# The order of weighing, projections and scores in a layer's attention

## The reference, cut to what matters

```
qkv = shift_tokens(x) @ Wqkv                 # 128 -> 3 * 1024: 16 heads of 64
q, k = l2norm(q) * qs, l2norm(k) * ksc       # then a rotation (rotary tables)
sim = einsum(q, k of this and the previous window of 32) * 8
attn = softmax(masked sim)
x = (attn @ v) @ Wo + x
x = ffn_layer(shift_tokens(x)) + x           # not touched
```

## Time and profile before

| what | us |
|---|---|
| median of 3 timed runs | 5682.57 |
| lowest, highest | 5681.54, 5702.88 |
| the profiled execution's own time | 5641.73 |
| its span, first to last instruction | 5639.9 |

### The profile page before, as it was taken

The page is one execution under the profiler, slowest core; times in us unless marked ns, Lnnn a source line. Parts: engine busy times, 40 slices in busy tenths (PEclk is TensorE's granted clock), DMA queues, the critical chain, the costliest instruction groups (busy, mean ns, idle before and its releaser), DMA issues. The chain is left out here.

```text
span 5639.9 us, 183409 instructions
## 1 busy us (share of the span) xinstructions
PE 4558.5 (81%) x70227; PEld 3064.2 (54%) x70227; DVE 3371.8 (60%) x7024; ACT 2396.0 (42%) x5161; POOL 2573.2 (46%) x4541
## 2 busy tenths in 40 slices
PE   8999838668888878888888888877788887888885
PEld 6777616544555545555555555555555555555553
DVE  3555441666666666665666666666566665666665
ACT  4555443124444344443444444444434444344441
POOL 0000000107666366663566645656546665366661
PEclk9999869879999999999999999989999999999998
DMA  1000003011111010101110111110101011011100
GB/s 34 4 4 3 1 0 98 6 37 28 26 25 29 24 33 22 29 22 30 26 29 22 28 30 26 24 27 22 37 19 29 22 28 37 19 24 27 28 22 31
DMA packets 76047, 143.02 MB, mean 25 GB/s; under 512 B 19655, under 2 KB 57749, under 8 KB 68117
## 3 DMA queue, kind: packets, MB, share of 16 engines
q1 hardware_dynamic: 75284, 131.92, 9.5%
HBM read 35.40 MB, written 4.19 MB: 7 GB/s over the span
## 5 line engine op out<-in xcount | busy, mean ns | idle before, releaser
L2439 DVE TENSOR_TENSOR n_tt<-n_pp,n_rot 128x1024 f32<-128x1024 f32 x768 | 923.4, 1222 | 693.4 <-ACT n_sq L2307 690.5
L1941 POOL TENSOR_TENSOR n_pre<-n_tt 128x512 f32<-128x512 f32 x768 | 969.9, 1274 | 802.8 <-DVE n_tt L2439 802.6
L2057 PE MATMUL n_pp<-n_wqkv,n_xT 128*128 128x512 f32 x1536 | 811.8, 631 | 6.3 <-ACT n_xT L2302 5.6
L2312 ACT COPY n_V<-n_pp 128x512 f32<-128x512 f32 x384 | 224.7, 585 | 1391.1 <-PE n_pp L2065 1391.1
L1976 POOL TENSOR_TENSOR n_pre<-n_pre,n_rn 128x512 f32<-128x512 f32 x768 | 776.6, 1042 | 36.8 <-POOL n_rn L1964 36.8
L2108 PE MATMUL n_pS<-n_qkT 64*32 64x64 f32 (+1 forms) x24576 | 359.4, 233 | 362.9 <-issue 362.9
L2307 ACT ACTIVATE n_sq<-n_pp 128x512 f32<-128x512 f32 x768 | 457.0, 595 | 158.5 <-PE n_pp L2057 152.8
L2108 PEld LDWEIGHTS n_pS<-n_qkT 64*32 64x32 f32 x24576 | 294.5, 110 | 396.2 <-issue 396.2
L2446 DVE TENSOR_REDUCE n_ss<-n_sq 128x8 f32<-128x512 f32 x768 | 504.2, 676 | 0.0
L2065 PE MATMUL n_pp<-n_wqkv,n_xT 128*64 128x512 f32 x1536 | 484.4, 760 | 0.0
L2074 PE MATMUL n_pp<-ident,n_pre 128*128 128x128 f32 x3072 | 420.7, 280 | 72.2 <-POOL n_pre L1976 70.2
(11 more groups left out here) (263 smaller groups left out, 7918.6 us busy)
## 6 DMA issues: line engine op xcount, KB each, us to landing
n_Vx<-n_V SPq DMA_DIRECT2D x192, 256.0 KB, 3.9
n_Vx<-n_V SPq DMA_DIRECT2D x192, 192.0 KB, 3.2
n_wqkv<-in_L_ffn_Wqkv SPq DMA_DIRECT2D x6, 1536.0 KB, 7.4
e_w<-in_L_ffn_w SPq DMA_DIRECT2D x32, 256.0 KB, 3.0
m_Y<-e_ye SPq DMA_DIRECT2D x64, 64.0 KB, 2.0
n_wo<-in_L_ffn_Wo SPq DMA_DIRECT2D x6, 512.0 KB, 7.2
a_xs<-in_L_attn_x SPq DMA_DIRECT2D x16, 128.0 KB, 2.1
x_kept<-X SPq DMA_DIRECT2D x1, 2048.0 KB, 8.6
```

The lines of the kernel that those rows point to most:

```text
L1941: nc.gpsimd.tensor_tensor(d, s[0], s[1][:, :, ::-1, :], ALU.add).then_inc(s_add, 1)
L2057: nc.tensor.matmul(pp[:, c % 2, :], xT[:, j * P:(j + 1) * P], wqkv[:, t * I + 512 * half:t * I + 512 * half + 512], start=True, stop=True) ...
L2439: nc.vector.tensor_tensor(tt[:, c % 4, :, :].rearrange("p s (h d) -> p s h d", d=D), bcast(pp[:, c % 2, :].rearrange("p (h d) -> p h d", d ...
```

## The change

In a half visit where the next visit exists (`nxt`), TensorE does weighing, two q/k projections, the wait for the turned q and k, two V projections and then the scores. The wait for `s_qkT` moves behind masks, weighing and the q/k projections there. ScalarE does both squares first, then the two V copies and the two exponentials. VectorE does the two rotations and one sum of squares ahead of the maxima, the second sum of squares behind them, and adds y to X after that. The number of instructions that compute is the same, GpSimd's and SyncE's lists are as before, and so are the banks.

```diff
--- before.py
+++ after.py
@@ -2173,18 +2173,20 @@
                         weights_ready(pairs[0], N, u, 0)
                     elif prev:
                         weights_ready(pairs[0], N - 1, 1 - u, 1)
-                    after(pe, s_qkT, 8 * N + 4 * j + 4)
+                    if not nxt:
+                        after(pe, s_qkT, 8 * N + 4 * j + 4)
                     masks(N, j)
                     if j == 1:
                         weigh(u, 0)
                     elif prev:
                         weigh(1 - u, 1)
-                    scores(j)
                     if nxt:
+                        project_qk(N + 1, 4 * j)
+                        project_qk(N + 1, 4 * j + 1)
+                        after(pe, s_qkT, 8 * N + 4 * j + 4)
                         project_v(N + 1, 2 * j, bank("v", 2 * j, 1))
                         project_v(N + 1, 2 * j + 1, bank("v", 2 * j + 1, 1))
-                        project_qk(N + 1, 4 * j)
-                        project_qk(N + 1, 4 * j + 1)
+                    scores(j)
                     if prev:
                         output(N - 1, j, bank("y", j, -1))
                     if j == 1:
@@ -2353,14 +2355,12 @@
 
                 for j in range(2):
                     if nxt:
+                        square(N + 1, 4 * j)
+                        square(N + 1, 4 * j + 1)
                         copy_v(N + 1, 1 - u, 2 * j, bank("v", 2 * j, 1))
                         copy_v(N + 1, 1 - u, 2 * j + 1, bank("v", 2 * j + 1, 1))
                     exps(N, j, 0)
-                    if nxt:
-                        square(N + 1, 4 * j)
                     exps(N, j, 1)
-                    if nxt:
-                        square(N + 1, 4 * j + 1)
                     if j == 1:
                         copy_output(N, 0, bank("o", 0, 0))
                         copy_output(N, 1, bank("o", 1, 0))
@@ -2494,15 +2494,15 @@
                         norm_output(N, 0)
                     elif prev:
                         norm_output(N - 1, 1)
-                    maxima(N, j)
                     if nxt:
                         rotate(N + 1, 4 * j)
                         rotate(N + 1, 4 * j + 1)
+                        sum_squares(N + 1, 4 * j)
+                    maxima(N, j)
+                    if nxt:
+                        sum_squares(N + 1, 4 * j + 1)
                     if prev:
                         add_attention(N - 1, b - 1, j, at["y", j, -1][0])
-                    if nxt:
-                        sum_squares(N + 1, 4 * j)
-                        sum_squares(N + 1, 4 * j + 1)
                     sum_exps(N, j)
                     if nxt:
                         for c in (4 * j + 2, 4 * j + 3):
```

## The result

The changed kernel takes 5330.45 us in the median of 4 runs (5325.95 to 5343.95), beside 5688.01 for the kernel before (5681.54 to 5702.88, 4 runs): a ratio of 0.9372, with a 95% interval of 0.9345 to 0.9398. Later, beside three variants on one chip, it took 5333.63 against 5680.34 (0.9391). The forecast was 5440, with 5300 to 5640; the saving is 357 us where 244 were forecast. Between the two profiled executions it is 316 us (5641.73 to 5325.95).

The account below looks back on a forecast made before the run. The prediction took TensorE's instruction supply, one block of 256 every 3.5 to 4 us, to limit the small matmuls. Terms -359 + 165 - 50 = -244 us gave 5440 us, range for 8 in 10: 5300 to 5640.

Parts of the forecast that it names:

- step (1): TensorE's scores: dense projections between weighing and scores remove the instruction-supply gap in 174 half visits, -359 us.
- C: Third of a loop iteration's four half visits, full clock and no loop end: 16.95 us before, forecast 15.55.
- step (2): TensorE's second turned output: new wait for VectorE's X, about 0.95 us in each half visit, 165 us lost.
- step (3): VectorE: two rotations and a sum of squares fit ahead of the maxima, 0.1 to 0.2 us to spare; cost nothing.
- The rival of the late maxima: VectorE's chain becomes the path: maxima 1 us late add 174 us, 5610; chance 0.13, plus 0.07 for over 1.2 us.
- step (4): ScalarE's squares first, earlier q/k projections, SyncE's copies and POOL (GpSimd): each costs nothing.
- step (5): TensorE's clock: B's low-clock loss of 1.3 us in each of 36 iterations goes, about -50 us; A's stays.
- B: Second of a loop iteration's four half visits, 20.97 us before, clock share 0.92; forecast to reach granted clock 1.00.
- A: First of a loop iteration's four half visits, behind the idle loop end, 20.17 us before; low-clock loss forecast unchanged.
- D: Fourth of a loop iteration's four half visits, 21.13 us before; gap in the scores forecast to go there too.

Follow-up runs that it names:

- run 72: Not a run number: 72 us is what adding y to X ahead of the second sum of squares saved against the changed kernel; 5261.86 us, ratio 0.9261.
- half of this change alone: Only TensorE's order changed against the kernel before, with VectorE and ScalarE keeping theirs: 5957.41 us, ratio 1.0512.
- one overlooked copy: Changed kernel with output y behind the turned outputs, so y waits for a ScalarE copy standing behind both exponentials: 5794.85 us, ratio 1.0198 to the kernel before.

## Why the prediction was right

**The supply gap, step (1).** Right, and shown by taking it away with useless work. I forecast -359 us, from the weight loads' idle time; the matmuls' own fell by 362.9 - 25.0 = 338, and that is what TensorE lost. Of the weight loads' own 396, 173 us are left at no cost to the matmuls. The count of 174 came out by luck: the change is in all but the last two half visits of a layer, and the first had no gap to lose.

The rule that I set against it stands in the Trainium skill, "Runtime: NRT & Kernel Launch", section "Instruction fetch mechanics": crossing a block is mostly hidden. For a run of small matmuls the traces do not agree: there are 2.1 us at C's crossing, and 1.7 us of filler take 363 us of such gaps down to 49. The same section of the Trainium skill says that a taken branch to code outside the two blocks at hand waits for a fetch. The trace agrees: with the loop written out, 90.2 us of idle time in 30 places go, 3.0 us each.

**The wait for X, step (2).** Right in mechanism; the path was not what I said. In C the second turned output was to start at 3.5 us and starts at 3.46; C was to take 15.55 us and takes 15.41. But I had all of the wait on the path, and in C hardly any of it is: with X earlier the wait fell by 0.6 us and C by 0.11. C's length is near the forecast because another chain, GpSimd's among it, ends there almost as late. Over the run 72 of 99 us came through. The waits themselves grew by 129 us (165.2 - 35.8) where I said 165.

**VectorE's cover, step (3).** It holds. From the masks the sum ends at 6.70 us (I said 6.8) and the scores at 7.11 (6.90), so there are 0.4 us to spare where I had 0.1 to 0.2, and VectorE waits 0.54 us where I gave 0 to 0.3. The sum itself took 0.68, not 0.60. The rival of the late maxima did not happen. That the other engines' orders are needed for it, the run of TensorE's order alone shows: 12% between them.

**ScalarE, SyncE, GpSimd, step (4).** Nothing in sum, as forecast, though not in each place: the turned weights in a layer's first visit wait 27 us for exponentials, which I had left out, and the wait of turned q and k for GpSimd fell by as much (70.2 to 41.8). And GpSimd's room in C was smaller than its busy time says: with four of its steps left out C falls, so the chain is on C's path, while its small chained steps idle between each other.

**The clock, step (5), mis-sized.** I gave 50 us for B and left A. The low level lost 948 - 713 = 235 us of time. The weighing's gaps fell by 10 us (91.6 to 81.2). What is left of the 316 us after the waits (316 - 338 + 129 - 10) is 97. TensorE's busy time for the same matmuls fell by about as much, 101.5 us (4558.5 to 4457.0), so most of the 97 is likely the clock; no run measures it apart. In B the granted clock was 0.92 and is 1.00, as I said, and A is still in part at the low level (0.75, now 0.83). I had sized B by one iteration. In the mean of 36, B spent 4.3 us at the low level before and none after, A 6.7 and 5.4, and the half visits at the start of a layer and D gave back some as well.

**A wait moved, not in my sum.** I had the gap in B's weighing stay at 1.44 us. It is 0.32 in the iteration shown, and in the mean 0.62 where it was 1.57; in D, where it was 0.11, it grew to 0.48, so the sum of these gaps hardly changed:

```profile
2251.00 0.30 PE L2133 MATMUL n_pW<-n_V,n_ET 64*32 64x64 f32 x4 [0.32 <-issue]
```

The changed kernel's own placing of the wait for turned q and k is worth about 34 us, as the run with that wait put back shows, and B's gap comes back with it. That TensorE reads ahead past the masks and so asks for its next block earlier is my reading of it; the run shows the gap and the price. These 34 us lie partly in the 10 and partly in the 97 above.

**From the profiled execution to the median.** I carried the saving over unchanged. The profiled run of the kernel before was its fastest: 34 runs of it, beside the experiments, lay between 5650 and 5697 us, and the four beside the first result between 5682 and 5703. Over the 34, for which the clock was listed, and the profiled one the time falls by 3.9 us for each 0.001 of granted clock (correlation -0.82), which is 0.35 us for each us at the low level. The profiled one had 0.916, all others but one 0.907 to 0.915. The changed kernel's profiled run is only 4.5 us below its median. So 41 of the 357 us lie in which run was profiled, and here the number was off for no fault of the mechanism. The saving is 113 us larger than forecast. These are 41 of it; the clock is 47 (97 against 50), the wait for X 36, the gaps in the weighing 10, and the supply gap takes 21 back.

## What to carry to other kernels

Count instructions as well as microseconds: where a list of small matmuls is longer than one block of 256 and quicker than the fetch of the next, put work of few, long instructions in the middle of it. Before an order is changed on one engine, follow each shared bank to the reader that frees it and to what stands ahead of that reader on its own engine; half of this change alone cost 5%, and one overlooked copy 8.6%. And idle time on TensorE can cost more than itself: 394 us more of waiting, 3.3 us at a time, came with a lower mean clock and cost 624.

## What the runs showed of the hardware

- A block of 256 of TensorE's instructions takes 3.45 to 4.02 us from one to the next when they are used up faster (57 pairs of gaps in the kernel before, median 3.75); 128 pairs of weight load and matmul on 64 x 32 tiles run in 1.29 to 1.45 us when the instructions are there.
- Adding 1440 matmuls of 0.21 us, from start to start, made the kernel 111 us faster.
- The end of a hardware loop on TensorE costs 2.7 to 3.3 us of idle time (89.3 us in 30 places in the kernel before), and with what goes with it, the lower clock in the half visit behind it above all, the loop cost 188 us in 30 ends, 6 us each (5280.12 to 5092.07, on two chips; 3.6% by ratio).
- A us at 1.2 GHz went with 0.35 us over the runs of the kernel before. TensorE's busy time, whose ends are modelled, moved by more: 101.5 us for 235 fewer us at that level in the changed kernel, and 261 for 525 more with TensorE's order alone.
- GpSimd's chained steps on 128 x 32 elements follow each other at 0.43 us, of which 0.18 to 0.20 are idle; 13 of them took 6.0 us in C of the changed kernel.
